# A two-layer attention and mixture-of-experts kernel: the second layer norm moved into the expert rounds, and the next stage's preparation into the last of them

## The chip, the cores and the metric

The kernel runs on one core of one Trainium2 chip. The metric is the device time of one execution in microseconds (us); lower is better. The engines are named as the profile names them: PE is TensorE's matmul, PEld its weight load, DVE is VectorE, ACT is ScalarE, POOL is GpSimd, SP is SyncE, which here only starts transfers.

## What is computed

The input X is 16 sequences of 256 rows of 128 numbers. Two layers are applied, each of the same form (cut from the reference):

```python
x = L0_attn_x
xn = _layernorm(x, axis=-1)
s = _L0_attn_ref(xn, L0_attn_w_in, L0_attn_w_out)
g = _silu(_L0_ffn_ref(xn, ...))          # 8 experts, 2 chosen per row, and a shared one
x = x + s * g
xn = _layernorm(x, axis=-1)              # the second layer norm
s = _L1_attn_ref(xn, Wq, bq, Wk, bk, Wv, bv, Wo, bo, rel_bias)
g = _silu(_L1_ffn_ref(xn, ...))          # two layers of window attention and a gated MLP
x = x + s * g
```

`_layernorm` is `(x - mean) / sqrt(var + 1e-5)` over the 128 numbers of a row. `_L1_attn_ref` has 16 heads of 8 numbers; it adds to the scores a bias that depends on the distance of query and key, clipped at 128, so the bias of all heads is a table of 256 x 256 per head.

## The kernel before

X and Y (the normalised rows) stay in SBUF as 32 tiles of 128 rows. Five stages follow one another, each a block in which every engine has a program of its own, written out by hand with semaphores; a block ends when all engines are done: `front` (first layer norm and router), `window_attention` (up to 262 us in the profile), `experts` (to 524 us), `normalise` (the second layer norm, to 533.5 us), `bias_attention` (to 909 us) and `inner_layers` (to the end).

**experts** works through 8 rounds of 512 rows (4 tiles). A round has 14 steps, one for each slice of 128 of the 1,760 hidden features (the last has 96). In a step, PE makes the gate product and the up product (three matmuls each, since every operand is split in a high and a low part) and, for the slice three steps back, the down product; ACT takes Silu of the gate (`e_sg`, L1202) and rounds the previous slice's product to its high part (`e_hh`, L1210); DVE multiplies `e_sg` by the router's share (L1243, steps 0 to 10 only; both inputs in SBUF) and with the up product in PSUM (L1247, which makes `e_h`); POOL makes the low part of `e_hh` (L1223; both inputs in SBUF). PE's up product of step s waits for `e_h` of step s-2, since they share a bank. At step 5 of a round DVE also updates the rows of the round before (L1250, L1253) and takes their statistics (L1257); at step 8 it splits the next round's input (L1231), which SP has fetched from Y. Rounds 1 to 6 stand in a hardware loop; round 0, round 7 and the rest after it (part 8, which updates the last 4 tiles) are written out.

**normalise** turns all 32 tiles' statistics into means and inverse deviations (L200 to L226) and then scales the 32 tiles, 16 on DVE (L454) and 16 on ACT (L445). Meanwhile SP loads the weights of the next stage and the bias table (4 MB in two transfers, L125).

**bias_attention** first transposes its weights and prepares constants (PE L839 to L844, ACT L929 and L931, DVE L984 to L996), then the first sequence's queries and keys (PE L852, L856; ACT L939 to L945; POOL L810, `a_kM`, the keys masked per head). Then it runs over 128 units of 4 heads x 128 queries x 256 keys: PE scores of two units (L884, into the four banks 0 to 3, so it waits until DVE has read them), DVE adds the table (L1004) and takes row maxima (L1008), POOL subtracts them (L816), ACT exponentiates, PE transposes and sums. A step of the written-out program is a unit; DVE and the scores work on even steps, two units at a time, four units ahead. Aux products run between: `x`, `qk`, `v` per sequence, `d` and `y` per tile (DVE L1015 and L1017 take the results).

Of the kernel before, what the change touches and what calls it, by code (L numbers as in the profile page):

```python
# [13 lines left out]
P = 128  # L14
# [63 lines left out]
def build_kernel(nc, t, out):  # L78
    ctx = ExitStack()
    with ctx:  # L80
# [6 lines left out]
        stats = ctx.enter_context(nc.sbuf_tensor("ln1_stats", [P, NT, 6], F32))  # L87
        with ExitStack() as early:
            S = early.enter_context(nc.sbuf_tensor("S0", [P, NT, P], F32))
            chosen = early.enter_context(nc.sbuf_tensor("chosen", [P, NT // 4, NE, 4], F32))  # L90
            wgu = early.enter_context(nc.sbuf_tensor("wgu", [P, 2, FEAT], F32))
            wd = early.enter_context(nc.sbuf_tensor("wd", [P, len(chunks(FEAT)), P], F32))
            experts_loaded = early.enter_context(nc.semaphore("experts_loaded"))

            with ExitStack() as first:
                sb = lambda n, s: first.enter_context(nc.sbuf_tensor("a0_" + n, s, F32))
                attn = {"wT": sb("wT", [P, 4, P]), "own": sb("own", [P, 4]), "table": sb("table", [P, TPB, H, 2 * WIN]),
                        "loaded": first.enter_context(nc.semaphore("a0_loaded"))}
                route = router_buffers(nc, first)
                front(nc, t, ps, X, Y, ident, wgu, wd, experts_loaded, skew, attn, route)  # L100
                window_attention(nc, "a0", t, ps, ident, Y, S, attn, lambda dve, part: choose_experts(nc, dve, part, route, chosen))
            experts(nc, t, ps, ident, X, Y, S, chosen, (wgu, wd, experts_loaded), stats)
        weights = inner_weights(nc, ctx)
        with ExitStack() as late:
            S = late.enter_context(nc.sbuf_tensor("S1", [P, NT, P], F32))
            table = late.enter_context(nc.sbuf_tensor("a1_table", [P, TPB, H, SEQ], F32))
            table_loaded = late.enter_context(nc.semaphore("a1_table_loaded"))
            attn = bias_weights(nc, late)
# [12 lines left out]
def load_bias_table(sp, skew, table, loaded):  # L121

    for tile in range(TPB):
        src = bass.AP(tensor=skew.tensor, offset=skew.offset + P * tile, ap=[[1, P], [512, H], [1, SEQ]])
        sp.dma_start(table[:, tile], src).then_inc(loaded, 16)  # L125
# [2031 lines left out]
```

## Time and profile before

| | |
|---|---|
| median of 3 runs | 1678.47 us (1676.99 to 1678.49) |
| the profiled execution | 1676.0 us, of which the profile's span is 1674.2 us |
| busy share of the span | PE 89%, DVE 79%, ACT 72%, POOL 66%, weight loads 69% |
| TensorE's granted clock, mean | 0.958 of 2.4 GHz |
| experts, 250 to 480 us | PE 213.8 of 230 us busy, DVE 149.1, POOL 123.6 |
| bias attention, 560 to 920 us | PE 332.3 of 360 us busy, DVE 321.1, POOL 288.8 |

A busy share is a mean over stages; what a change in one stage costs has to be read from the rows of that stage. Times in rows are in us from the start of the span unless marked ns. "Idle before" names how long the engine had waited and what ended the wait.

### The profile page before, as it was taken

Reading aid. Unit: us, or ns where it says so; the run is one execution under the profiler, and the core shown is the slowest. Engines: PE = TensorE matmul, PEld = TensorE weight load, DVE = VectorE, ACT = ScalarE, POOL = GpSimd, SP = SyncE. Lnnn points to the kernel's source line nnn. Section 1 sums busy time; section 2 is a strip of 40 time slices with the busy share of each in tenths; the row PEclk is TensorE's granted clock in tenths of the full one; section 3 lists DMA queues with packets and bytes.
Section 4 is the critical chain, followed back from the end, with each engine's and each line's share of the span. In section 5 each row is a group of like instructions: output and inputs, shape, how many; then the busy total and the mean of one; then the engine's idle time right before and its main releaser. Section 6 shows DMA issues by size and latency. Waiting matters only on the chain. (4 is left out here: it accounts for less than half of the span.)

```text
span 1674.2 us, 43938 instructions
## 1 busy us (share of the span) xinstructions
PE 1482.3 (89%) x16870; PEld 1161.5 (69%) x16870; DVE 1321.7 (79%) x2179; ACT 1212.5 (72%) x2057; POOL 1100.9 (66%) x659
## 2 busy tenths in 40 slices
PE   6899996999995899999997588999999999989885
PEld 5577774888883566666665377777777777777774
DVE  4898884667665999999996888888888888888753
ACT  2677774555554688888886488888888888888863
POOL 2677761666663788888886576776677766766615
PEclk7899997999997899999998799999999999999997
DMA  5000004333323200000000001011111111111113
GB/s 175 2 4 3 3 3 124 113 97 106 99 69 113 78 2 14 2 14 2 14 2 23 10 21 34 22 26 28 27 27 27 27 27 24 27 27 27 24 24 107
DMA packets 66432, 66.79 MB, mean 40 GB/s; under 512 B 26252, under 2 KB 46256, under 8 KB 65984
## 3 DMA queue, kind: packets, MB, share of 16 engines
q1 hardware_dynamic: 66240, 64.13, 13.7%
q8 instruction: 132, 2.16, 0.5%
q14 instruction: 60, 0.49, 0.1%
HBM read 40.69 MB, written 4.36 MB: 27 GB/s over the span
## 5 line engine op out<-in xcount | busy, mean ns | idle before, releaser
L816 POOL TENSOR_TENSOR a_prob<-a_prob,a_top 128x1024 f32<-128x1024 f32 x128 | 239.7, 1894 | 48.3 <-DVE a_top L1008 48.3
L1223 POOL TENSOR_TENSOR e_hh<-e_h,e_hh 128x512 fp32r<-128x512 f32 x112 | 148.8, 1329 | 121.4 <-ACT e_hh L1210 121.2
L1491 POOL TENSOR_TENSOR i_qk<-i_qk,i_rt 128x1024 f32<-128x1024 f32 x64 | 152.0, 2374 | 39.4 <-DVE i_rt L1940 35.0
L1501 POOL TENSOR_TENSOR i_qk<-i_qk,i_rn 128x1024 f32<-128x1024 f32 x64 | 122.5, 1915 | 79.9 <-DVE i_rn L1919 79.9
L1796 ACT ACTIVATE i_prob<-i_prob,i_top 128x128 f32<-128x128 f32 x512 | 156.4, 392 | 17.2 <-DVE i_top L1928 15.3
L1004 DVE TENSOR_TENSOR a_prob<-ps,a_table 128x1024 f32<-128x1024 f32 x128 | 149.7, 1211 | 23.0 <-PE ps L884 21.0
L962 ACT ACTIVATE a_probT<-ps 128x1024 f32<-128x1024 f32 x128 | 131.1, 1025 | 44.5 <-PE ps L892 44.5
L892 PEld LDWEIGHTS ps<-ident,a_prob 128*128 128x128 f32 x1024 | 112.8, 141 | 64.2 <-ACT a_probT L962 50.7
L1488 POOL TENSOR_TENSOR i_qk<-i_raw,i_rot 128x1024 f32<-128x1024 f32 x59 | 140.2, 2376 | 23.8 <-issue 23.8
L1008 DVE TENSOR_REDUCE a_top<-a_prob 128x4 f32<-128x1024 f32 x128 | 149.4, 1208 | 0.0
L892 PE MATMUL ps<-ident,a_prob 128*128 128x128 f32 x1024 | 138.3, 278 | 6.0 <-ACT a_probT L962 1.6
L537 POOL TENSOR_TENSOR a_prob<-a_prob,a_top 128x1024 f32<-128x1024 f32 x64 | 120.2, 1897 | 26.2 <-DVE a_top L690 26.2
L1202 ACT ACTIVATE e_sg<-ps 128x512 f32<-128x512 f32 x112 | 66.8, 597 | 96.0 <-PE ps L1129 95.2
L957 ACT ACTIVATE a_prob<-a_prob 128x1024 f32<-128x1024 f32 x128 | 135.5, 1058 | 0.6 <-POOL a_prob L816 0.6
L1761 ACT ACTIVATE i_raw<-ps 128x1024 f32<-128x1024 f32 x64 | 65.6, 1025 | 76.1 <-PE ps L1558 75.9
L1247 DVE TENSOR_TENSOR e_h<-ps,e_sg 128x512 f32<-128x512 f32 x112 | 77.5, 692 | 41.6 <-PE ps L1129 27.0
L1127 PE MATMUL ps<-e_xT,e_wgu_hi 128*128 128x512 f32 x224 | 90.1, 402 | 10.7 <-DVE e_wd_lo L1269 10.7
L1243 DVE TENSOR_TENSOR e_sg<-e_sg,e_share 128x512 f32<-128x512 f32 x88 | 68.1, 773 | 33.5 <-ACT e_sg L1202 32.8
L1129 PE MATMUL ps<-e_xT,e_wgu_lo 128*128 128x512 f32 x224 | 89.1, 398 | 0.0
L1128 PE MATMUL ps<-e_xT,e_wgu_hi 128*128 128x512 f32 x224 | 88.5, 395 | 0.0
L1637 PE MATMUL ps<-i_wo,i_oT 128*128 128x128 f32 x512 | 71.0, 283 | 19.6 <-ACT i_oT L1807 19.6
L1940 DVE TENSOR_TENSOR i_rt<-ps,i_rot 128x512 f32<-128x512 f32 x128 | 81.9, 682 | 6.4 <-ACT i_raw L1761 6.4
(297 smaller groups left out, 4296.7 us busy)
## 6 DMA issues: line engine op xcount, KB each, us to landing
i_V<-i_V SPq DMA_DIRECT2D x96, 130.0 KB, 2.3
e_share<-chosen_scratch SPq DMA_DIRECT2D x32, 256.0 KB, 3.2
a_table<-skew_scratch SPq DMA_DIRECT2D x2, 2048.0 KB, 12.4
e_share<-chosen_scratch SPq DMA_DIRECT2D x16, 224.0 KB, 2.9
e_share<-chosen_scratch SPq DMA_DIRECT2D x16, 192.0 KB, 2.7
e_share<-chosen_scratch SPq DMA_DIRECT2D x16, 160.0 KB, 2.5
X<-in_L_attn_x SPq DMA_DIRECT2D x4, 512.0 KB, 5.9
a_table<-in_c_l_table SPq DMA_DIRECT2D x1, 2048.0 KB, 7.9
```

The source lines that it names most:

```text
L537: nc.gpsimd.tensor_tensor(s, s, top[:, slot].unsqueeze(2).broadcast_to([P, HG, KW]), ALU.subtract).then_inc(shifted, 1)
L816: nc.gpsimd.tensor_tensor(s, s, top[:, slot].unsqueeze(2).broadcast_to([P, HG, KW]), ALU.subtract).then_inc(shifted, 1)
L892: last = nc.tensor.transpose(ps[:, 4 + b // 4, b % 4 * P:(b % 4 + 1) * P], flat[:, b * P:(b + 1) * P], ident[:, :])
L957: nc.scalar.activation(s, s, ACT.Exp).then_inc(exped, 1)
L962: nc.scalar.activation(probT[:, n % 4].rearrange('p (b n) -> p b n', b=2), ps[:, 4:6, :], ACT.Copy).then_inc(pT_sb, 1)
L1004: nc.vector.tensor_tensor(prob[:, slot].rearrange('p (b x) k -> p b x k', b=2), ps[:, 2 * (n % 2):2 * (n % 2) + 2, :].rearrange('p b (x k) ...
L1008: nc.vector.tensor_reduce(top[:, slot], prob[:, slot], AX.X, ALU.max).then_inc(max_done, 1)
L1223: nc.gpsimd.tensor_tensor(low, h[0:n, slot(b, parity, HBUF), :], high.bitcast(F32), ALU.subtract).then_inc(h_lo, 1)
L1488: nc.gpsimd.tensor_tensor(s, raw[:, T % 2], cosines, ALU.mult).then_inc(cos_done, 1)
L1491: nc.gpsimd.tensor_tensor(s, s, rt[:], ALU.add).then_inc(rotated, 1)
L1501: nc.gpsimd.tensor_tensor(flat, flat, rn[:, T // TPB % 2, T % TPB].unsqueeze(2).broadcast_to([P, 2 * FH, FD]), ALU.mult).then_inc(qk_done, 1)
L1796: last = nc.scalar.activation(s, s, ACT.Exp, bias=top[:, T % 2, h:h + 1])
```

## The change

1. `normalise` is gone. In `experts`, DVE keeps statistics of the 4 tiles of one round only; it takes them at step 6, turns them into variances and a first guess of the inverse deviation at step 7, refines the guess three times (twice at step 11, once at step 12: nine operations on 4 numbers a partition) and scales the four tiles at steps 12 and 13, all for the round before, in rounds 1 to 7. The first guess is now an integer trick on DVE, no longer Ln and Exp on ACT.
2. The last 4 tiles are normalised inside `bias_attention`, on DVE, at its steps 21, 23 and 25.
3. The weights and half the bias table are loaded in round 0 of the experts, over the room of the experts' raw weights, which are no longer needed there. In round 7 PE, ACT, DVE and POOL prepare the constants, the first sequence's queries and keys and `a_kM`.
4. `bias_attention` begins with the first scores (its step -4); the table's other half is loaded at its start.

The core of the diff (loads in `bias_weights`, names, and the parts removed from `bias_attention`, which the list above names, are cut):

```diff
+def small_variances(nc, dve, stats, mv, var, rstd):
+
+    for k in range(4):
+        nc.vector.bn_aggr(mv[:, k, :], stats[:, k, :])
+    dve.drain()
+    nc.vector.tensor_scalar(var[:], mv[:, :, 1], 1e-5, None, ALU.add)
+    dve.drain()
+    nc.vector.tensor_scalar(rstd[:].bitcast(I32), var[:].bitcast(I32), -0.5, RSQRT_MAGIC, ALU.mult, ALU.add)
+    dve.drain()
+
+
+def small_refinement(nc, dve, var, rstd, tmp):
+
+    nc.vector.scalar_tensor_tensor(tmp[:], var[:], -0.5, rstd[:], ALU.mult, ALU.mult)
+    dve.drain()
+    nc.vector.tensor_tensor(tmp[:], tmp[:], rstd[:], ALU.mult)
+    dve.drain()
+    nc.vector.scalar_tensor_tensor(rstd[:], tmp[:], 1.5, rstd[:], ALU.add, ALU.mult)
+    dve.drain()
...
@@ bias_attention @@
+        LAST_ROWS = 21
+        JOBS = sorted([(i * U + AT[kind], 0, kind, i, 0) for i in range(NBATCH) for kind in AT if i or kind == 'v'] + ...
...
         def _(sp):
-            sp.wait_ge(w_loaded, NWL)
-            sp.wait_ge(b_loaded, NBL)
+            load_bias_tile(sp, skew, 1, tile1[:], table_loaded)
             loads(sp)
...
+                if step == LAST_ROWS:
+                    small_variances(nc, dve, stats, mv, var, rstd)
+                    small_refinement(nc, dve, var, rstd, tmp)
+                if step == LAST_ROWS + 2:
+                    small_refinement(nc, dve, var, rstd, tmp)
+                    small_refinement(nc, dve, var, rstd, tmp)
+                if step == LAST_ROWS + 4:
+                    for k in range(4):
+                        r = NT - 4 + k
+                        last = nc.vector.tensor_scalar(Y[:, r, :], X[:, r, :], mv[:, k, 0:1], rstd[:, k:k + 1], ALU.subtract, ALU.mult)
+                    last.then_inc(last_rows, 1)
...
@@ experts, SP, after the shares of round 0 @@
+            sp.wait_ge(w_hi, 2)
+            sp.wait_ge(w_lo, 3)
+            load_bias_weights(sp, t, attn)
+            load_bias_tile(sp, skew, 0, attn["tile0"], attn["table_loaded"])
             with sp.Fori(1, ROUNDS) as i:
...
@@ experts, PE, in round 7 @@
+                if s == 1:
+                    pe.wait_ge(attn["w_loaded"], BIAS_LOADS)
+                    for j in range(4):
+                        last = nc.tensor.transpose(ps[:, TURNED, j * P:(j + 1) * P], wnat[:, j, :], ident[:, :])
...
+                elif s == OUT:
+                    pe.wait_ge(prep_sb, 2)
+                    nc.tensor.matmul(ps[:, TURNED, P:2 * P], bvT, wT[:, 3, :], start=True, stop=True).then_inc(prep_ps, 1)
+                    for k in range(TPB):
+                        last = nc.tensor.transpose(ps[:, 7, k * P:(k + 1) * P], Y[:, k, :], ident[:, :])
...
+                elif s == FETCH:
+                    pe.wait_ge(prep_sb, 3)
+                    for j, turned in enumerate((xT1, xR1)):
+                        last = nc.tensor.matmul(ps[:, 7, j * SEQ:(j + 1) * SEQ], wT[:, j, :], turned[:, 0, :], start=True, stop=True)
...
@@ experts, POOL, in round 7 @@
+                        if ending(i) and b == FETCH + 1:
+                            pool.wait_ge(prep_sb, 4)
+                            nc.gpsimd.tensor_tensor(kM1[:, 0], kT1[:, :].unsqueeze(1).broadcast_to([P, 4, SEQ]),
+                                                    own.unsqueeze(2).broadcast_to([P, 4, SEQ]), ALU.mult)
...
@@ experts, DVE @@
+                    if s == OUT + (exists(i) and 1) and exists(i - 1):
                         for k in range(4):
-                            nc.vector.bn_stats(stats[:, bass.ds(i * 4 - 4 + k, 1), :], X[:, bass.ds(i * 4 - 4 + k, 1), :])
+                            nc.vector.bn_stats(stats[:, k, :], X[:, bass.ds(i * 4 - 4 + k, 1), :].rearrange("p k e -> p (k e)"))
+                    if exists(i) and exists(i - 1):
+                        if s == OUT + 2:
+                            dve.drain()
+                            small_variances(nc, dve, stats, mv, var, rstd)
+                        elif s in (NR, NR + 1):
+                            small_refinement(nc, dve, var, rstd, tmp)
+                            if s == NR:
+                                small_refinement(nc, dve, var, rstd, tmp)
+                        if s in (NR + 1, NR + 2):
+                            for k in range(2):
+                                q = 2 * (s - NR - 1) + k
...
+                                nc.vector.tensor_scalar(to, own_rows, mv[:, q, 0:1], rstd[:, q:q + 1], ALU.subtract, ALU.mult)
```

In this code OUT is 5, FETCH is 8 and NR is 11.

The order of instructions shows where these land. On DVE in round 7, around the update of the previous round's rows (steps 5 to 8), the kernel before has:

```order
L1250 TENSOR_TENSOR e_upd<-ps,S 128x512 [waits e_out_T]
L1253 TENSOR_TENSOR X<-X,e_upd 128x512
L1257 BN_STATS ln_stats<-X 128x6 x4
L1243 TENSOR_TENSOR e_sg<-e_sg,e_share 128x512 [waits e_share_in1,e_gate_sb]
L1247 TENSOR_TENSOR e_h<-ps,e_sg 128x512 [waits e_h_lo,e_up_ps]
L1243 TENSOR_TENSOR e_sg<-e_sg,e_share 128x512 [waits e_gate_sb]
L1247 TENSOR_TENSOR e_h<-ps,e_sg 128x512 [waits e_h_lo,e_up_ps]
```

and the changed kernel:

```order
L1281 TENSOR_TENSOR e_upd<-ps,S 128x512 [waits e_out_T]
L1284 TENSOR_TENSOR X<-X,e_upd 128x512
L1274 TENSOR_TENSOR e_sg<-e_sg,e_share 128x512 [waits e_share_in1,e_gate_sb]
L1278 TENSOR_TENSOR e_h<-ps,e_sg 128x512 [waits e_h_lo,e_up_ps]
L1289 BN_STATS ln_stats<-X 128x6 x4
L1274 TENSOR_TENSOR e_sg<-e_sg,e_share 128x512 [waits e_gate_sb]
L1278 TENSOR_TENSOR e_h<-ps,e_sg 128x512 [waits e_h_lo,e_up_ps]
L436 BN_AGGR e_mv<-ln_stats 128x2 x4
L438 TENSOR_SCALAR e_var<-e_mv 128x4
L440 TENSOR_SCALAR e_rstd<-e_var 128x4
L1274 TENSOR_TENSOR e_sg<-e_sg,e_share 128x512 [waits e_gate_sb]
L1278 TENSOR_TENSOR e_h<-ps,e_sg 128x512 [waits e_h_lo,e_up_ps]
```

The statistics moved behind the share multiply and `e_h` of step 6, and the variances stand behind `e_h` of step 7.

On DVE at the end of the same round (steps 11 to 13), where the kernel before had three `e_h` operations and nothing between them, the changed kernel has:

```order
L1278 TENSOR_TENSOR e_h<-ps,e_sg 128x512 [waits e_h_lo,e_up_ps,e_gate_sb]
L446 SCALAR_TENSOR_TENSOR e_tmp<-e_var,e_rstd 128x4
L448 TENSOR_TENSOR e_tmp<-e_tmp,e_rstd 128x4
L450 SCALAR_TENSOR_TENSOR e_rstd<-e_tmp,e_rstd 128x4
L446 SCALAR_TENSOR_TENSOR e_tmp<-e_var,e_rstd 128x4
L448 TENSOR_TENSOR e_tmp<-e_tmp,e_rstd 128x4
L450 SCALAR_TENSOR_TENSOR e_rstd<-e_tmp,e_rstd 128x4
L1278 TENSOR_TENSOR e_h<-ps,e_sg 128x512 [waits e_h_lo,e_up_ps,e_gate_sb]
```

After these come three more small operations and two scalings, the `e_h` of step 13 and two more scalings, in each of the seven rounds.

On PE at the start of `bias_attention`, the kernel before has:

```order
L835 UNCONDITIONAL_BRANCH [waits barrier_Pool_Activation_PE_DVE_SP_release]
L839 MATMUL ps<-ident,a_wnat 128x128 [waits a1_w_loaded]
L839 MATMUL ps<-ident,a_wnat 128x128 x3
L842 MATMUL ps<-ident,a_bvo 128x128 [waits a1_b_loaded]
L844 MATMUL ps<-a_wT,a_bvT 128x128 [waits a1_wT_sb]
L852 MATMUL ps<-ident,Y 128x128 [waits a1_wO_sb]
L852 MATMUL ps<-ident,Y 128x128
L856 MATMUL ps<-a_xT,a_wT 128x256 [waits a1_aux_free]
L856 MATMUL ps<-a_xR,a_wT 128x256
L884 MATMUL ps<-a_kM,a_qT 128x512 [waits a1_aux_free,a1_masked]
```

and the changed kernel:

```order
L818 UNCONDITIONAL_BRANCH [waits barrier_Pool_Activation_PE_DVE_SP_release]
L860 MATMUL ps<-a_kM,a_qT 128x512 x4
L837 MATMUL ps<-a_wT,a_xR 128x128 x2
L860 MATMUL ps<-a_kM,a_qT 128x512 [waits a1_biased]
L860 MATMUL ps<-a_kM,a_qT 128x512 x3
L827 MATMUL ps<-ident,Y 128x128 [waits a1_aux_free]
```

The first scores stand right behind the release of the block and wait for nothing.

## Rows read from the trace of the kernel before

**Rows 1.** Timeline from the end of the experts to the first scores and their use: start us, us, engine, line.

```profile
524.42 0.21 DVE L200 TENSOR_TENSOR ln_mean<-ln_stats 128x32 f32<-128x32 f32 x1 [0.30 <-PEq L1051]
...
527.27 6.26 ACT L445 ACTIVATE Y<-X,ln_shift,ln_rstd 128x128 f32<-128x128 f32 x16 [1.06 <-DVE ln_shift L226]
...
543.58 2.09 PE L884 MATMUL ps<-a_kM,a_qT 32*128 32x512 f32 x8 [2.63 <-POOL a_kM L810]
...
545.81 2.36 DVE L1004 TENSOR_TENSOR a_prob<-ps,a_table 128x1024 f32<-128x1024 f32 x2 [8.46 <-PE ps L884]
```

**Rows 2.** Window of PE's last work in the experts: length, busy us (count) of PE, PEld, DVE, ACT, POOL, granted clock, DMA share, GB/s.

```profile
520.00:524.00 4.00, 0.98 (x6) 0.42 (x4) 2.14 (x6) 0.60 (x1) 0.00 (x0) 0.94 0.00 0
```

**Rows 3.** Timeline of POOL, DVE and PE in steps 5 to 12 of one expert round.

```profile
381.70 1.30 POOL L1223 TENSOR_TENSOR e_hh<-e_h,e_hh 128x512 fp32r<-128x512 f32 x1 [1.22 <-ACT e_hh L1210]
381.78 0.98 DVE L1257 BATCH_NORM_STATS2 ln_stats<-X  x4 [0.19 <-issue]
382.69 0.86 DVE L1243 TENSOR_TENSOR e_sg<-e_sg,e_share 128x512 f32<-128x512 f32 x1
...
384.45 0.50 PE L1127 MATMUL ps<-e_xT,e_wgu_hi 128*128 128x512 f32 x1
...
387.14 0.69 DVE L1247 TENSOR_TENSOR e_h<-ps,e_sg 128x512 f32<-128x512 f32 x1 [0.16 <-issue]
...
389.12 0.40 PE L1127 MATMUL ps<-e_xT,e_wgu_hi 128*128 128x512 f32 x1
...
394.25 0.69 DVE L1247 TENSOR_TENSOR e_h<-ps,e_sg 128x512 f32<-128x512 f32 x1 [1.40 <-PE ps L1129]
```

**Rows 4.** Timeline of DVE and POOL in the inner layers, where small DVE operations meet POOL.

```profile
933.80 2.34 POOL L1491 TENSOR_TENSOR i_qk<-i_qk,i_rt 128x1024 f32<-128x1024 f32 x1 [2.31 <-DVE i_rt L1940]
933.99 2.20 DVE L1917 TENSOR_TENSOR i_rtmp<-i_rtmp,i_rn 128x32 f32<-128x32 f32 x1
936.26 0.19 DVE L1919 SCALAR_TENSOR_TENSOR i_rn<-i_rtmp,i_rn 128x32 f32<-128x32 f32 x1
```

**Rows 5.** Two DVE lines over the whole run: duration ns least/median/most, first and last start.

```profile
L1998 DVE TENSOR_SCALAR i_var<-i_mv x16: 169/170/753, 1015.2 to 1644.5; 128x4 f32<-128x4 f32 x16
...
L2019 DVE TENSOR_SCALAR i_G<-i_ms,i_mv,i_rstd x60: 330/338/1176, 1024.2 to 1628.1; 128x128 f32<-128x128 f32 x60
```

**Rows 6.** Timeline of DVE near the end: the same small operations with POOL idle.

```profile
1644.09 0.38 DVE L1996 BATCH_NORM_AGGREGATE i_mv<-i_st 128x2 f32<-128x6 f32 x4
1644.55 0.17 DVE L1998 TENSOR_SCALAR i_var<-i_mv 128x4 f32<-128x4 f32 x1
...
1645.12 0.17 DVE L2012 SCALAR_TENSOR_TENSOR ps<-ps,i_rstd 128x4 f32<-128x4 f32 x1
1645.37 0.17 DVE L2014 TENSOR_TENSOR ps<-ps,i_rstd 128x4 f32<-128x4 f32 x1
...
1647.31 1.12 DVE L2019 TENSOR_SCALAR i_qk<-i_ms,i_mv,i_rstd 128x128 f32<-128x128 f32 x4
```

**Rows 7.** Timeline of POOL and DVE in the steady part of the bias attention.

```profile
603.24 3.74 POOL L816 TENSOR_TENSOR a_prob<-a_prob,a_top 128x1024 f32<-128x1024 f32 x2
...
605.85 2.33 DVE L1008 TENSOR_REDUCE a_top<-a_prob 128x4 f32<-128x1024 f32 x2
...
609.63 2.36 DVE L1004 TENSOR_TENSOR a_prob<-ps,a_table 128x1024 f32<-128x1024 f32 x2 [0.81 <-PE ps L884]
```

**Rows 8.** Timeline of PE: transposes in an expert round, and products of queries and keys.

```profile
378.49 0.60 PE L1153 MATMUL ps<-ident,e_gT 128*128 128x128 f32 x4
...
599.67 0.70 PE L856 MATMUL ps<-a_xT,a_wT 128*128 128x256 f32 x2
```

**Rows 9.** Timeline of DVE and ACT in round 0.

```profile
276.43 0.28 DVE L1269 TENSOR_TENSOR e_wd_lo<-wd,e_wd_hi 96x128 fp32r<-96x128 f32 x1
...
295.58 0.60 ACT L1190 ACTIVATE e_xT<-ps 128x512 fp32r<-128x512 f32 x1 [0.54 <-PE ps L1135]
```

**Rows 10.** The page's DMA issues: count, KB each, median us from issue to landing.

```profile
a_table<-skew_scratch SPq DMA_DIRECT2D x2, 2048.0 KB, 12.4
```

More of the change, by code:

```diff
@@ L86, in build_kernel @@
         skew = nc.dram_tensor("skew_scratch", (H, 512), F32, kind="Internal").ap()
[L87 to L108, printed above, removed]
-            normalise(nc, "ln1", X, Y, stats, lambda sp: (load_bias_weights(sp, t, attn), load_bias_table(sp, skew, table, table_loaded)))
-            bias_attention(nc, "a1", t, ps, ident, Y, S, attn, (table, table_loaded),
-                           lambda sp: load_inner_weights(sp, t, weights), kept)
+        stats = ctx.enter_context(nc.sbuf_tensor("ln1_stats", [P, 4, 6], F32))
@@ L717, in _, with bias_attention @@
                     between(dve, 1 + step // 8)
-def bias_attention(nc, name, t, ps, ident, Y, S, attn, bias=None, loads=None, kept=None):
+def bias_attention(nc, name, t, ps, ident, X, Y, S, stats, skew, attn, loads, kept):
     KW = SEQ
@@ L836, in _ @@
         def _(pe):
-            pe.wait_ge(w_loaded, NWL)
-            for j in range(4):
-                last = nc.tensor.transpose(ps[:, 0, j * P:(j + 1) * P], wnat[:, j, :], ident[:, :])
-            last.then_inc(wT_ps, 1)
-            pe.wait_ge(b_loaded, NBL)
-            nc.tensor.transpose(ps[:, 1, 0:P], bvo[:, 0, :], ident[:, :]).then_inc(wT_ps, 1)
-            pe.wait_ge(wT_sb, 2)
-            nc.tensor.matmul(ps[:, 2, 0:P], bvT[:, :], wT[:, 3, :], start=True, stop=True).then_inc(wT_ps, 1)
-            pe.wait_ge(wO_sb, 5)
             def job(n, kind, i, tile):
@@ L1064, in experts @@
         upd = sb("upd", [P, 4, P])
+        rows = gT[:, 0:2 * P].rearrange("p (v t) -> p v t", v=2)
+        mv, var, rstd, tmp = sb("mv", [P, 4, 2]), sb("var", [P, 4]), sb("rstd", [P, 4]), sb("tmp", [P, 4])
+        wnat, own, bqk, bvo, pick, bvT, parity_of, wT, wO, xT1, xR1, qT1, kT1, kM1 = (attn[n] for n in (
+            "wnat", "own", "bqk", "bvo", "pick", "bvT", "parity", "wT", "wO", "xT", "xR", "qT", "kT", "kM"))
         (rows_T, rows_sb, rows_out, w_hi, w_lo, staged, x_T, x_hi, x_lo, gate_ps, up_ps, gate_sb, shared_out, h1, h_hi,
```

209 lines of the change are left out of this document (120 added, 89 removed).

## The prediction

> **What bounds the kernel now.** I read four views, in this order. The timeline around the end of the experts shows the gap that the change wants to close: the next block's first instruction stands at 524.42, the scaling of the tiles fills ACT until 533.5, and the first scores start at 543.58, behind the preparation; DVE can add the bias at 545.81 [rows 1]. Between 524.4 and 543.6 nothing of the 128 units is done, so this stretch is on the path whole. The timeline of an expert round shows the price side. PE is never idle there: 14 steps of about 2.08 us and two sets of transposes make a round of 30.1. DVE has some 0.5 us to spare in a step with the share multiply and 1.40 in each of steps 11 to 13 [rows 3]. But in steps 6 to 10 it has nothing to spare: it is late by the update of step 5, and PE's up product of step 8 already comes 0.1 late (a first matmul of 0.50 where others take 0.40). `e_h` of step 8 ends at 387.83, and the up product that needs it starts at 389.12: 1.3 us of margin [rows 3]. In the bias attention DVE is the bound: two adds and two maxima take 4.6 us a pair of units, reciprocals and outputs 0.6 more, of a period of 5.5 (63 pairs between 545.8 and 891); it waits 0.81 us on one pair in two [rows 7].
>
> The third thing to see is how DVE and POOL meet. An operation on 32 numbers a partition, with both inputs in SBUF, took 2.20 us when POOL's multiply had started 0.19 before it, and ended 0.05 after POOL's did; its like took 0.19 with POOL idle [rows 4]. A sum on 4 numbers took 753 ns against 170, a scaling of 128x128 up to 1176 against 338 [rows 5]. The share multiply of step 6 took 0.86 instead of 0.69, because POOL had begun at 381.70 [rows 3]. So operations with two SBUF inputs, and scalings from SBUF to SBUF, stand still while POOL works. Operations that read PSUM, and the statistics, do not: 381.78 to 382.69 of statistics ran under POOL's 1.30 [rows 3].
>
> **What the change gives.** The first scores move from 543.58 to the start of the block, 524.45: **-19.1 us**. The adds follow at the same distance. PE's clock: its mean was 0.94 in 520 to 524, so it fell to 1.2 GHz just before 524 [rows 2], and the first scores run at 1.2 GHz before and after; no gain and no loss. POOL's clearing of V and ACT's table load move with the block and end before the first maxima exist. The table's first half is long there.
>
> **PE's preparation in round 7**: seven transposes at 0.10 to 0.15 us (four took 0.60 busy), one product like them, and two products of 256 columns (0.70 for the first) [rows 8], on an engine without idle time: **+2.0**.
>
> **The norm in rounds 1 to 7, on DVE.** Operations without POOL: aggregates 0.46, two sums 0.25 each, nine refinements at 0.25 apart, four scalings at 0.28 [rows 6], with drains 4.6 us a round. Two stretches:
> - Steps 6 to 10. The statistics, 0.9 us, stood in the shadow of POOL's operation; the share multiply of step 6 now meets POOL instead and ends when it did before, at 383.55, and the 0.9 comes on top. The variances add 1.05 at step 7, and one of their two sums meets POOL, about 1.1. Of 3.05, the margin of 1.3 takes part; PE loses 1.75.
> - Steps 11 to 13. Nine refinements and four scalings are 3.5 us. All wait for POOL, which has one operation of 1.3 per step; a wait of about 1.1 comes once for each of POOL's four operations from step 11 to the next round's step 0: 4.4. Free are 3 x 1.4 = 4.2 and a margin of some 2 us before PE's up products wait. 7.9 - 4.2 - 2.0 leaves 1.7.
>
> That is 3.5 a round, **+24.5** for seven. The bounds: nothing, if the waits fall between POOL's operations, and 5.0 a round, if more of the share multiplies, pushed out of their rhythm, meet POOL as well. I take 3.5, since the rows of steps 6 to 10 leave DVE no place to catch up.
>
> The Trainium skill, "VectorE: DVE Perf Modes", section "The TRN2 errata — SBUF-src ops pay a fixed extra latency per instruction", tabulates VectorE's SBUF operations at 58 cycles plus the elements, an estimate of 0.065 us for four numbers. By it eleven small operations a round would cost 2.0 us less than by their distance of 0.25 in rows 6, 14 us over seven rounds, and the whole sum would come out near +6. The trace decides here, with 0.17 us each and 0.25 apart [rows 6].
>
> **DVE's and POOL's preparation in round 7**: a fill, seven small copies, sums and scalings, 1.8 us in all, of which three meet POOL (3 x 1.1), and on POOL one more `a_kM` of the size of a subtraction, 1.9, in step 9. Of this 5 to 7 us the free 0.5 a step takes part: **+4** (0 to 7).
>
> **The last four tiles in the bias attention, on DVE.** 4.5 us of operations at the distances of rows 6. Each of the three places follows a pair of maxima, when POOL has just begun its two subtractions, 3.74 us in one piece [rows 7]. POOL starts them after the first maximum, DVE is done with the second 1.1 later, and then stands for the rest, less what fits between the two: about 2.1 a place, 6.3. DVE's own waits of 0.81 before the adds give back 2.4. **+8.4** (2 to 11).
>
> **Transfers.** SP's ten new transfers wait for DVE's splitting, which ends at 276.7; round 1's input is used at 295.6 [rows 9]. Nine small loads, the table of 2 MB and the input behind it fit into 19 us, since two such tables took 12.4 each to land when issued together [rows 10]. The second half starts at 524.4 and is needed at the fifth unit, 9 us after the first add, near 536. Both at nothing; late, they would cost up to 5.
>
> **The sum**: -19.1 + 2.0 + 24.5 + 4 + 8.4 = +19.8. On the profiled execution's 1676.0 that is 1695.8; the median of the runs shown is 2.5 above it. I predict **1697**, slower.
>
> **The rivals.**
> - **The small operations cost nothing** (faster). If they fall into POOL's pauses and DVE's spare time carries them, what remains is -19.1 + 2.0 and 2.1 for the last tiles: -15, 1662. For it: DVE is busy only 149 of 230 us in the experts. Against it: the busy share is not where the waits are, rows 3. It decides at the price of a round: with the other terms as above, below 0.7 us a round the change is faster; with those halved, below 1.5. Chance 0.15.
> - **Only the first stretch costs.** Steps 11 to 13 absorb theirs: 7 x 1.75 = 12, in place of 24.5, and 2 for the preparation: +5, 1681 to 1684. For it: 1.40 us free in each of the three steps. Chance 0.2, a quarter of it within 0.2% of no change.
> - **A transfer is late**: round 1's input or the second half of the table, up to 5 us over the forecast, 1702. Chance 0.05.
> - **The gap does not close**: the first adds wait for something else than the preparation, as the clearing of V or the landing of a table, and only some 10 us are won: 1706. For it: the rows show no execution in which the preparation is missing. Against: POOL waited for `a_kM`'s input, and PE for `a_kM` [rows 1]. Chance 0.05.
> - The forecast has the remaining 0.55.
>
> The Trainium skill, "SBUF — State Buffer", section "Who interferes with whom", says that VectorE and GpSimd share a pair of ports under an exclusive lock, that an instruction with two SBUF inputs or in a two-port mode takes it, and that the later one stands for the whole of the other's instruction. By that rule the sum is the +19.8; without it the price of a round falls to the 4.6 us of work, and the first rival comes near. The trace agrees with the rule: 2.20 against 0.19 us [rows 4].
>
> **The range.** Low, the second rival: 1680. High, 5.0 a round and the full 11 for the last tiles: 1696 + 10.5 + 2.6 with some of the late transfer, 1711. That leaves out the first rival and little else. 0.2% is 3.4 us, about what a measurement of this kernel can tell from no change. Faster by more 0.15, within it 0.05, slower by more 0.80.
>
> **What would show it.** In the changed profile: the first scores about 0.1 us after the last statistics of the experts (gain right); rounds 1 to 6 of 33 to 34 us where they were 30.1, with PE waiting for `e_h` at steps 9 to 10 and at the round's start; refinements of four numbers with a longest time over 1 us and a mean well above 0.17; the share multiply of step 6 near 1.7 us; the distance from the first add to the last one 6 to 11 us longer. Rounds of 30.5 or less would make the forecast wrong, and then most likely the sign. If the small operations show 0.17 us throughout, the waits for POOL were misjudged; if they wait but the rounds do not grow, it is the margins.

## The result, and the profile after

| | before | after |
|---|---|---|
| median of all runs shown | 1678.48 us (1676.99 to 1679.82) | 1692.22 us (1689.45 to 1693.08) |
| ratio, with its 95% interval | | 1.0079 [1.0062, 1.0097] |
| profiled execution, its span | 1676.0, 1674.2 | 1689.45, 1687.7 |
| DVE busy, POOL busy | 79%, 66% | 82%, 65% |

The changed kernel is slower by 0.8%, 13.7 us between the medians and 13.5 between the profiled executions. The forecast was 1697, with 1680 to 1711 as its range. The head of the changed kernel's page:

```profile
PE 1491.2 (88%) x16870; PEld 1164.3 (69%) x16870; DVE 1377.8 (82%) x2304; ACT 1205.8 (71%) x2039; POOL 1104.2 (65%) x659
```

**The gap closed.** The timeline of the changed kernel at the end of the experts, to be set against [rows 1] (start us, us, engine, line):

```profile
544.16 0.60 ACT L1204 ACTIVATE e_gT<-ps 128x512 f32<-128x512 f32 x1 [2.94 <-PE ps L1112]
544.81 1.11 PE L1136 MATMUL ps<-ident,e_gT 128*128 128x128 f32 x4 [0.69 <-ACT e_gT L1204]
...
548.79 2.09 PE L860 MATMUL ps<-a_kM,a_qT 32*128 32x512 f32 x8 [2.86 <-PEq L1019]
...
551.01 2.35 DVE L961 TENSOR_TENSOR a_prob<-ps,experts_then_bias 128x1024 f32<-128x1024 f32 x2 [2.53 <-PE ps L860]
```

The last Silu of the experts in the kernel before, where the same stretch began:

```profile
520.36 0.60 ACT L1197 ACTIVATE e_gT<-ps 128x512 f32<-128x512 f32 x1 [2.65 <-PE ps L1129]
```

From the experts' last Silu to the first scores it is now 4.63 us, and was 23.22 (520.36 to 543.58): 18.6 won. The first add follows the scores at 2.2 us, as before.

**The rounds grew.** The gate's Silu that opens rounds 2 and 3, in the kernel before and after:

```profile
337.54 0.60 ACT L1202 ACTIVATE e_sg<-ps 128x512 f32<-128x512 f32 x1 [1.04 <-PE ps L1129]
367.65 0.60 ACT L1202 ACTIVATE e_sg<-ps 128x512 f32<-128x512 f32 x1 [1.03 <-PE ps L1129]
```

```profile
341.68 0.58 ACT L1209 ACTIVATE e_sg<-ps 128x512 f32<-128x512 f32 x1
374.56 0.58 ACT L1209 ACTIVATE e_sg<-ps 128x512 f32<-128x512 f32 x1
```

Round 2, of 30.11 us, has become one of 32.88. Measured so for every round, and cut at the events that both kernels have, the 13.5 us come from these places:

| stretch | before | after | difference |
|---|---|---|---|
| to the first gate of round 0 (same code) | 278.62 | 280.82 | +2.2 |
| rounds 0 to 6 | 209.37 | 224.64 | +15.3 |
| round 7, to the last output's Silu | 32.37 | 38.70 | +6.3 |
| to the first scores | 23.22 | 4.63 | -18.6 |
| first add to last add of the bias attention | 345.32 | 355.62 | +10.3 |
| last add to the end (same code) | 783.1 | 781.0 | -2.1 |

The first and the last stretch are code that the change leaves alone. Over the profiles of all kernels of this document the first lies between 273.8 and 281.8 us and the last between 780.9 and 785.5, so nothing shows that the +2.2 and the -2.1 come from the change.

**Where a round loses.** Two places. Steps 6 to 10 of round 3 in the changed kernel, to be set against [rows 3]:

```profile
389.38 1.29 POOL L1250 TENSOR_TENSOR e_hh<-e_h,e_hh 128x512 fp32r<-128x512 f32 x1 [1.23 <-ACT e_hh L1217]
389.52 1.69 DVE L1274 TENSOR_TENSOR e_sg<-e_sg,e_share 128x512 f32<-128x512 f32 x1 [0.26 <-issue]
...
391.98 0.86 DVE L1289 BATCH_NORM_STATS2 ln_stats<-X 128x6 f32 x4
...
395.03 1.29 POOL L1250 TENSOR_TENSOR e_hh<-e_h,e_hh 128x512 fp32r<-128x512 f32 x1 [0.44 <-ACT e_hh L1217]
395.08 1.27 DVE L440 TENSOR_SCALAR e_rstd<-e_var 128x4 int32<-128x4 int32 x1
...
397.35 0.69 DVE L1278 TENSOR_TENSOR e_h<-ps,e_sg 128x512 f32<-128x512 f32 x1 [0.16 <-issue]
...
398.10 0.50 PE L1110 MATMUL ps<-e_xT,e_wgu_hi 128*128 128x512 f32 x1 [1.13 <-DVE e_h L1278]
```

The share multiply of step 6 takes 1.69 where it took 0.86, because it now meets POOL's operation, which the statistics met before. The integer guess of step 7, four numbers, stands 1.27 for the whole of POOL's 1.29. PE, which never waited in the rounds before the change, waits 1.13: this is the up product of step 10, which needs the `e_h` of step 8. And the end of that round:

```profile
402.54 2.54 POOL L1250 TENSOR_TENSOR e_hh<-e_h,e_hh 128x512 fp32r<-128x512 f32 x2 [0.41 <-ACT e_hh L1217]
402.66 1.19 DVE L448 TENSOR_TENSOR e_tmp<-e_tmp,e_rstd 128x4 f32<-128x4 f32 x1 [0.20 <-issue]
403.93 1.18 DVE L450 SCALAR_TENSOR_TENSOR e_rstd<-e_tmp,e_rstd 128x4 f32<-128x4 f32 x1
...
407.44 1.68 DVE L1303 TENSOR_SCALAR Y<-X,e_mv,e_rstd  x2
407.49 1.29 POOL L1250 TENSOR_TENSOR e_hh<-e_h,e_hh 128x512 fp32r<-128x512 f32 x1 [2.41 <-ACT e_hh L1217]
409.04 0.68 DVE L1278 TENSOR_TENSOR e_h<-ps,e_sg 96x512 f32<-96x512 f32 x1
...
409.77 0.50 PE L1110 MATMUL ps<-e_xT,e_wgu_hi 128*128 128x512 f32 x1 [0.62 <-DVE e_h L1278]
```

Two of the nine refinement operations and one of the scalings stand for POOL; the `e_h` of step 13 is late and PE's up product waits 0.62 for it in the next round's step 1. Over all rounds the small operations took 21.4 us more than they would at their shortest durations, the scalings 7.6, the share multiplies 16.1 (8.1 before the change).

### The profile page after: what moved, and what is told of

It is laid out like the page before. It is cut to its first block and busy times, and to the rows that moved or that the text cites. A ratio compares the mean times of both kernels' runs of the same rounds, so it can differ in the third digit from the quotient of the medians.

```text
span 1687.7 us, 44126 instructions
## 1 busy us (share of the span) xinstructions
PE 1491.2 (88%) x16870; PEld 1164.3 (69%) x16870; DVE 1377.8 (82%) x2304; ACT 1205.8 (71%) x2039; POOL 1104.2 (65%) x659
## 5 line engine op out<-in xcount | busy, mean ns | idle before, releaser
L1217 ACT ACTIVATE e_hh<-e_h 128x512 fp32r<-128x512 f32 x112 | 70.5, 630 | 68.8 <-DVE e_h L1278 66.4
L1274 DVE TENSOR_TENSOR e_sg<-e_sg,e_share 128x512 f32<-128x512 f32 x88 | 75.4, 856 | 14.8 <-ACT e_sg L1209 12.0
```

## The experiments

In all of them the theory is that DVE's waits for POOL make the price of the moved norm; the rivals say what else could. Times are medians, each ratio with its 95% interval is against the kernel before on the same chip, and a "round" is the distance between first gates, taken from the run's profile.

### Small operations over PSUM; no norm in the rounds

`e1_psum_rounds`, in `experts`:

```diff
-        mv, var, rstd, tmp = sb("mv", [P, 4, 2]), sb("var", [P, 4]), sb("rstd", [P, 4]), sb("tmp", [P, 4])
+        mv, rstd = sb("mv", [P, 4, 2]), sb("rstd", [P, 4])
+        var, tmp = ps[:, GATED, 0:4], ps[:, GATED, 4:8]
```

> The changed kernel, but in the expert rounds the variance and the temporary of four numbers lie in PSUM (bank 4, after the update has read it), so that none of the eleven small operations has two SBUF operands; the scalings stay as they are. In the changed kernel the small operations of the rounds stood 21 us in all beyond their shortest durations, the scalings 7.6, the share multiplies 8. Theory (waits for POOL make the price of a round): no small operation of the rounds above 0.25 us, rounds 1 to 6 fall from 32.7 to between 30.8 and 31.8, the kernel is 7 to 13 us shorter, 1680 to 1685. Rival (the added work is the price, not the waits, or the waits fall where they cost nothing): rounds within 0.4 of 32.7, 1689 to 1692.

Measured: 1674.11 us, 0.9985 [0.9971, 0.9998], rounds 2 to 6 of 31.15 (32.75 in the changed kernel), round 7 of 34.15 (38.70). The same lines of the two kernels over the whole run (duration ns least/median/most), first the changed kernel, then this one:

```profile
L440 DVE TENSOR_SCALAR e_rstd<-e_var x7: 170/1273/1274, 329.4 to 525.4; 128x4 int32<-128x4 int32 x7
L448 DVE TENSOR_TENSOR e_tmp<-e_tmp,e_rstd x21: 161/164/1190, 337.3 to 537.9; 128x4 f32<-128x4 f32 x21
```

```profile
L440 DVE TENSOR_SCALAR e_rstd<-ps x7: 161/163/164, 324.5 to 510.9; 128x4 int32<-128x4 int32 x7
L448 DVE TENSOR_TENSOR ps<-ps,e_rstd x21: 170/171/171, 332.0 to 520.6; 128x4 f32<-128x4 f32 x21
L450 DVE SCALAR_TENSOR_TENSOR e_rstd<-ps,e_rstd x21: 161/163/165, 332.3 to 520.9; 128x4 f32<-128x4 f32 x21
```

The same operations, in the same number and place, with one operand in another memory: none waits any more (the share multiplies and the scalings still do), and the rounds fall as the theory said. Most of the price was not their work but their waits. The kernel's gain is larger than expected: round 7 gives back 4.5 us and not 1.6, of which below, and of the 15.2 us between the two profiled executions 4.9 stand ahead of the first gate, where the code is the same.

`e2_no_norm_rounds` leaves out the small operations and the scalings in the rounds, so its result is not normalised:

```diff
-                    if exists(i) and exists(i - 1):
+                    if False:
                         if s == OUT + 2:
```

> The changed kernel without the small operations and the scalings of the second norm in the expert rounds (the first 28 tiles are not normalised); the statistics stay at step 6, the preparation in round 7 and the last four tiles stay. Theory: rounds 1 to 6 are back near 30.1 (30.1 to 30.6), round 7 is near 35, the kernel 18 to 20 us shorter, 1671 to 1675. Rival (the move of the statistics from step 5 to step 6, out of the shadow of POOL's operation, costs by itself the 0.9 us a round of the prediction): rounds near 31.0, 1678 to 1680.

Measured: 1668.55 us, 0.9953 [0.9936, 0.9969]; rounds 1 to 5 of 30.11 or 30.12 and round 7 of 34.16. The time lies below the expected 1671 to 1675, the rounds are as the theory had them. The whole growth of the rounds is that of the small operations and scalings, and the moved statistics alone cost nothing: a share multiply still takes up to 1.70 us there, but within the margin. The run also gives the preparation's own price: 34.16 - 32.37 = 1.8 us.

### Statistics back at step 5

`e6_stats_step5`:

```diff
-                    if s == OUT + (exists(i) and 1) and exists(i - 1):
+                    if s == OUT and exists(i - 1):
```

> The changed kernel with the statistics of a round back at step 5, where they stood before the change. The run without the norm had rounds of 30.12 with the statistics at step 6, so alone their move costs nothing. Theory A (it costs 0.9 us a round together with the variances, as the prediction had it: the share multiply of step 6 meets POOL's operation behind the update, and with statistics ahead of it that wait was hidden): rounds 1 to 6 fall by 0.7 to 1.0, to 31.7 to 32.0, the kernel 5 to 7 us shorter. Rival B (DVE recovers it before PE notices; the price comes from the waits of the small operations and scalings alone): rounds within 0.3 of 32.7.

Measured: 1682.47 us, 1.0027 [1.0013, 1.0041], rounds 2 to 6 of 31.00, a gain of 1.75 a round and more than either said. The integer guess at step 7 now meets POOL in one round of seven, not in six. All the small operations together still wait 17 us over the run, where it was 21: it is above all the place of a wait that has changed. What remains is the late end of the round alone: from the gate of step 0 to that of step 1 it is 3.05 us where it was 2.01, and from step 9 to step 10 it is 2.08 again (3.67 in the changed kernel). Round 7 gains nothing by it: it takes 39.88 us, and 38.70 in the changed kernel.

### The last four tiles

`e4_no_last_tiles`:

```diff
-                    if i >= NBATCH - 4 // TPB:
-                        pe.wait_ge(last_rows, 1)
...
-                if step == LAST_ROWS:
-                    small_variances(nc, dve, stats, mv, var, rstd)
-                    small_refinement(nc, dve, var, rstd, tmp)
...
```

> The changed kernel without the norm of the last four tiles (those are not normalised), and nothing else. Theory: from the first add to the last 345.3 us as before the change, the kernel 9 to 11 us shorter, 1681 to 1683. Rival (part of the 10.3 us comes from something else in the bias attention, as the halves of the table lying in two buffers or the later start of a transfer): the distance stays above 348 and the gain below 7.

Measured: 1679.16 us, 1.0012 [1.0000, 1.0023]; first to last add 345.33 us (345.32 before the change). The 10.3 us are these operations' whole; the kernel's time is 2 us below the expected 1681 to 1683. How they lose is in the changed kernel's timeline:

```profile
618.61 3.75 POOL L800 TENSOR_TENSOR a_prob<-a_prob,a_top 128x1024 f32<-128x1024 f32 x2 [1.83 <-DVE a_top L965]
...
620.02 0.51 DVE L438 TENSOR_SCALAR a_var<-a_mv 128x4 f32<-128x4 f32 x1
620.61 1.77 DVE L440 TENSOR_SCALAR a_rstd<-a_var 128x4 int32<-128x4 int32 x1
...
636.31 3.74 POOL L800 TENSOR_TENSOR a_prob<-a_prob,a_top 128x1024 f32<-128x1024 f32 x2
637.12 3.02 DVE L994 TENSOR_SCALAR Y<-X,a_mv,a_rstd 128x128 f32<-128x128 f32 x2
```

A blocked operation gets in when one of POOL's two subtractions ends, and the next one may be blocked by the second: the sum that makes the variance ends at 620.53, when the second subtraction has begun, and the guess behind it ends at 622.38, with that subtraction (618.61 + 3.75 = 622.36). Two scalings of 0.33 took 3.02.

`e5_last_tiles_before_maxima` puts the same three blocks (at steps 22, 24, 26) between the adds and the maxima:

```diff
                 if step % 2 == 0 and 0 <= n < UNITS:
                     add_bias(n, n % NBUF)
                     add_bias(n + 1, (n + 1) % NBUF)
+                if step == LAST_ROWS:
+                    small_variances(nc, dve, stats, mv, var, rstd)
+                    small_refinement(nc, dve, var, rstd, tmp)
...
                 if step % 2 == 0 and 0 <= n < UNITS:
                     row_max(n, n % NBUF)
```

> The changed kernel with the norm of the last four tiles in three places as before, but each between the second add of a pair and its first maximum, where POOL's two subtractions are nearly at their end, instead of behind the second maximum, where they have just begun. Same operations, same number in each place. Theory (the waits for POOL make over half of the 10.3 us of the bias attention): the waits fall from 6.8 us to under 1.5, the distance from the first to the last add is 348.5 to 350.5 (the work of 4.5 less some free time), the kernel 5 to 7 us shorter, 1685 to 1687. Rival (the work and its place in DVE's row is the price): the distance stays above 354.

Measured: 1684.66 us, 1.0044 [1.0026, 1.0061]; first to last add 350.51, within the expectation. The waits are 1.9 us, not under 1.5: POOL's `a_kM` was in the way once.

```profile
623.43 1.89 POOL L794 TENSOR_TENSOR a_kM<-a_kT,experts_then_bias 128x1024 f32<-128x1024 f32 x1
623.57 1.77 DVE L448 TENSOR_TENSOR a_tmp<-a_tmp,a_rstd 128x4 f32<-128x4 f32 x1
```

`e3_last_tiles_first` does all of it ahead of DVE's first add:

```diff
+            small_variances(nc, dve, stats, mv, var, rstd)
+            for _ in range(3):
+                small_refinement(nc, dve, var, rstd, tmp)
+            for k in range(4):
...
+            last.then_inc(last_rows, 1)
             dve.wait_ge(table_loaded, 16)
```

> The changed kernel with the norm of the last four tiles in one piece at the start of the bias attention, ahead of DVE's first add, where DVE is idle for 2.3 us and POOL only clears V. The same 4.5 us of DVE work. Theory (in the old place 6.8 us of waits for POOL's subtractions come on top of the 4.5 of work): the first add is 2 to 4 us later, the distance from the first to the last add falls from 355.6 to about 345.5, the kernel is 6 to 8 us shorter, 1684 to 1686. Rival (the work costs, not the waits; the clearing of V holds DVE just as the subtractions do): first add 5 us or more later, 1688 or more.

Measured: 1685.73 us, 1.0046 [1.0028, 1.0065]; first to last add 345.55, the first add 3.7 us later. The gain is 6.4 of the 10.3. POOL's clearing of V does hold DVE, as the rival had it, but only one operation of it: the variance, with one SBUF input.

```profile
549.83 2.23 POOL L786 MEMSET a_V<- 128x2560 f32 x1 [6.26 <-POOLq L1015]
549.88 0.38 DVE L436 BATCH_NORM_AGGREGATE a_mv<-ln_stats 128x2 f32<-128x6 f32 x4 [0.31 <-PEq L1015]
550.34 1.75 DVE L438 TENSOR_SCALAR a_var<-a_mv 128x4 f32<-128x4 f32 x1
```

### The remedies together

`e7_psum_spread` is `e1` with the last tiles' work in six pieces, one on every second pair of units, between adds and maxima:

```diff
+                if step == LAST_ROWS:
+                    small_variances(nc, dve, stats, mv, var, rstd)
+                if step in (LAST_ROWS + 4, LAST_ROWS + 8, LAST_ROWS + 12):
+                    small_refinement(nc, dve, var, rstd, tmp)
+                if step in (LAST_ROWS + 16, LAST_ROWS + 20):
...
```

> Small operations of the rounds over PSUM, and the norm of the last four tiles spread over six pairs of units in the bias attention, each piece between the adds and the maxima (variances, then three times one refinement, then twice two scalings, every second pair). Theory: rounds of 31.16 as in the run with PSUM, round 7 of 34.15, and the six pieces of 0.7 to 1.05 us go mostly into the 0.81 that DVE waits on one pair in two: distance from first to last add 345.5 to 348, and the kernel 7 to 10 us shorter than with PSUM alone, 1664 to 1668, faster than before the change by 10 or more. Rival (each place delays the next maximum and POOL after it, whatever its size): distance above 350, 1669 or more.

Measured: 1667.35 us, 0.9945 [0.9925, 0.9965]; rounds of 31.14, first to last add 347.0. The operations still wait 3.5 us for POOL there, but together with their work they cost 1.7 us; that DVE's free 0.81 us on one pair in two [rows 7] takes the rest is the reading, not tested by itself.

`e8_psum_spread_act` takes the scalings from DVE, which computes a shift instead, and adds on ACT:

```diff
+                    if s == NR + 2 and exists(i) and exists(i - 1):
+                        act.wait_ge(refined, i)
+                        for q in range(4):
...
+                            nc.scalar.activation(to, own_rows, ACT.Identity, bias=shift[:, q:q + 1], scale=rstd[:, q:q + 1])
```

> As the kernel with PSUM and spread pieces, and the four scalings of a round on ACT (Y = X * rstd + shift) at step 13 behind its copy, two small PSUM operations more on DVE. That takes 1.35 us of scalings and 0.83 of their waits from DVE in each round and puts four activations of some 0.3 us on ACT. Theory (what is left of the rounds' price, 1.04 us a round, is DVE being late through the scalings and the share multiplies that meet POOL behind them): rounds fall to between 30.1 and 30.6, the kernel 4 to 7 us shorter than without ACT's part, 1658 to 1663. Rival (ACT, with two activations of 1.2 us in a step of 2.08, becomes late by four more in one step and delays POOL's input and PE): rounds of 31.2 or more.

Measured: 1672.43 us, 0.9966 [0.9952, 0.9980]; rounds of 31.16. The theory fell: with the statistics at step 6, what is left of a round's price is not in the scalings. The median is 5 us above that of `e7`. From the first gate of the experts to their last Silu it is 250.6 us against 249.6, 1.0 longer; in the profiled executions most of the rest stands in the unchanged code at both ends. The rival's reason, that ACT delays PE, does not account for the rounds either, since with the statistics at step 5 (the next two runs) ACT's part leaves them at 30.1.

`e9_psum_stats5_spread` is `e7` with the edit of `e6`; `e10_psum_stats5_spread_act` is `e8` with it.

> As the kernel with PSUM and spread pieces, and the statistics of a round back at step 5. Measured so far, per round over the 30.11 of before: 2.65 with both as in the change, 0.9 with the statistics at step 5 alone, 1.05 with PSUM alone. Theory A (two lateness terms that add: the share multiply of step 6 meets POOL when the statistics don't stand between, and the small operations meet it later): both remedies together leave 0 to 0.3, rounds 30.1 to 30.4, the kernel 5 to 7 us shorter than with the statistics at step 6, 1659 to 1663. Rival B (both cure the same lateness, and what is left is the added work of DVE in steps 5 to 8): rounds stay at 30.8 to 31.2, 1665 to 1668.

Measured: 1664.59 us, 0.9919 [0.9896, 0.9941], rounds 1 to 5 of 30.11 to 30.15: the norm is in the rounds and costs nothing there. That is theory A for the rounds; the time lies 1.6 us above its range, and round 7, of 35.99 us, is 1.8 longer than in `e7` (34.19).

> As the run before it, and the four scalings on ACT at step 13. With the statistics at step 6 ACT's part changed the rounds by +0.05 us (31.19 against 31.14), so steps 11 to 13 hold no price once the small operations do not wait. Theory A: rounds within 0.15 of the run before it, time the same within 2 us. Rival B (the scalings, with 0.83 us of waits a round, are what is left of the price when steps 5 to 8 are cured): rounds 0.3 or more shorter, down to 30.1.

Measured: 1663.99 us, 0.9924 [0.9903, 0.9946], rounds 2 to 6 of 30.11 to 30.15. Theory A again: ACT's part does neither good nor harm in these rounds. At the end of round 7 it helps: from the last gate to the last Silu it is 5.57 us (6.51 in `e9`), and the experts from first gate to last Silu are 0.9 shorter, too little to see in the medians.

PE's first product of each gate and up set and its waits for `e_h`, from 280 to 480 us, in the changed kernel, in `e7` and in `e9`, one fence each (count; busy us, mean ns; idle us before and the releaser):

```profile
L1110 PE MATMUL ps<-e_xT,e_wgu_hi 128*128 128x512 f32 (+1 forms) x175 | 71.6, 409 | 9.5 <-DVE e_h L1278 9.3
```

```profile
L1111 PE MATMUL ps<-e_xT,e_wgu_hi 128*128 128x512 f32 (+1 forms) x183 | 73.3, 400 | 4.0 <-DVE e_h L1279 4.0
```

```profile
L1111 PE MATMUL ps<-e_xT,e_wgu_hi 128*128 128x512 f32 (+1 forms) x187 | 75.0, 401 | 0.0
```

The mean of rounds 2 to 6 in the four combinations (30.09 before the change):

| | small operations over SBUF | over PSUM |
|---|---|---|
| statistics at step 6 | 32.75 | 31.15 |
| statistics at step 5 | 31.00 | 30.10 |

So there are two latenesses, and PE's own waits for `e_h` show where each falls. In a round of the changed kernel PE waits 1.13 us at step 10, and 0.13 to 0.31 and 0.64 at steps 0 and 1 of the next round. In `e1` the second wait is gone and 0.8 of the first is left; in `e6` the first is gone and 0.5 to 0.64 of the second is left; in `e9` there is none. The late end of the round costs 0.9 by itself (31.00 - 30.10), the steps 6 to 10 cost 1.05 by themselves (31.15 - 30.10), with two share multiplies that meet POOL (1.69 and 1.49 us in a round of `e1`). Both together cost 2.65, and the 0.7 above the sum belongs to neither alone: with the statistics at step 6 the guess meets POOL as well, and PE waits longer at both places.

**Round 7.** In `e9` its end is late by itself: 6.51 us from the last gate to the last Silu (4.76 before the change, 8.66 in the changed kernel), with two scalings of 2.63 us ahead of the last `e_h`. `e11_early_in_round_7` moves that round's refinements and scalings one step forward:

```diff
-                        elif s in (NR, NR + 1):
+                        elif s in (NR - ending(i), NR + 1 - ending(i)):
...
-                        if s in (NR + 1, NR + 2):
+                        if s in (NR + 1 - ending(i), NR + 2 - ending(i)):
```

> As the kernel with PSUM, statistics at step 5 and spread pieces, and in round 7 alone the refinements and scalings one step earlier (steps 10 to 12 in place of 11 to 13). In that kernel's round 7 the time from the last gate on ACT to the last output's Silu was 6.51 us where it was 4.76 before the change, because two scalings, together 2.63 us in place of 0.6, stood ahead of the last product of step 13. Theory (what is late at the end of the experts goes onto the path whole): that time is 4.8 to 5.2 again, round 7 falls from 36.0 to 34.2 to 34.6, the kernel some 1.5 us shorter, 1661 to 1665. Rival (POOL's row is late by itself there, through the masking of the keys in step 9): the time stays at 6.0 or more.

Measured: 1663.15 us, 0.9918 [0.9896, 0.9940], but that time is 6.84: the theory fell. By the rows, the masking of the keys is in POOL's row there, POOL works nearly without a pause behind it, and the scalings meet it one step earlier instead, which is what the rival had:

```profile
514.82 1.90 POOL L1254 TENSOR_TENSOR a_kM<-a_kT,experts_then_bias 128x1024 f32<-128x1024 f32 x1
...
516.67 2.54 POOL L1251 TENSOR_TENSOR e_hh<-e_h,e_hh 128x512 fp32r<-128x512 f32 x2
...
517.33 1.97 DVE L1304 TENSOR_SCALAR Y<-X,e_mv,e_rstd 128x128 f32<-128x128 f32 x2
519.22 0.68 DVE L1279 TENSOR_TENSOR e_h<-ps,e_sg 128x512 f32<-128x512 f32 x1
```

What removes these last 2 us of round 7 was not found. Two runs point at ways that were not tried: in `e1` and `e7`, with the norm and the masking in round 7 but the statistics at step 6, this time is 4.76 and 4.80, so round 7 alone could keep its statistics there; and with the scalings on ACT (`e10`) it is 5.57. `e9`, `e10` and `e11` cannot be told apart by their times; each beats the kernel before by 0.8%. Of the 18.6 us that the closed gap gives, `e9` keeps 13: round 7 takes 3.6 and the last tiles 1.7.

## Why the prediction was right, term by term

| term | predicted | measured |
|---|---|---|
| first scores move | -19.1 | -18.6 |
| PE's preparation, and DVE's and POOL's | +2.0 and +4 | +1.8 for both |
| norm in seven rounds | +24.5 | +19.8 (15.3 in rounds 1 to 6 and, in round 7, 4.5) |
| last four tiles | +8.4 | +10.3 |
| transfers | 0 | 0 |
| unchanged code | 0 | +2.2 and -2.1 |
| sum | +19.8 | +13.5 |

- **The number.** The sum was 6.3 us too high: the preparation was put 4.2 too high, the norm 4.7, the last tiles 1.9 too low. The larger errors went the same way, towards too slow; the measured 1692 lies in the range, 5 us below the forecast. The 2.5 us between the profiled execution and the median was added only by half (1695.8 became 1697 and not 1698).
- **The sign** rested on one reading: that small SBUF operations stand for POOL, and that rows of steps 6 to 10 leave DVE no place to catch up. Both held. By PSUM against SBUF (`e1`) and by place against place (`e5`, `e6`, `e9`) it was the waits and not the work. The rival "small operations cost nothing" is what `e9` is, by another arrangement: 1664.6, where the rival was priced at 1662.
- **First stretch, 1.75 a round**: taking the statistics back to step 5 gives 1.75 (`e6`), but that the two numbers are equal is luck: with the small operations over PSUM the same move gives 1.05. The details came as told: the share multiply of step 6 at 1.69 (forecast "near 1.7"), the guess of step 7 waiting 1.1, PE waiting for `e_h` at step 10. The 0.9 of the statistics costs nothing alone (`e2`), as the prediction's own margin of 1.3 would have it. What it did not see is that the statistics' place also decides whether the guess, or the share multiply of step 8, meets POOL; so taking them back gave more than 0.9.
- **Second stretch, 1.7 a round**: 0.9 in rounds 1 to 6 if the first stretch is cured (31.00 against 30.10), 1.6 if it is not (32.75 against 31.15). Both stretches together were put at 3.5 and measured 2.65, and this is the mis-sized term. The step that was off was "a wait of about 1.1 comes once for each of POOL's four operations": in the rows of round 3 three operations waited (1.0, 1.0 and 1.1 beyond their own durations), 3.1 us in place of 4.4.
- **Round 7** went the other way: the norm cost 4.5 there where 3.5 was forecast. Of this 3.9 stand behind the last gate (4.76 us before, 8.66 after, from last gate to last Silu): behind the last `e_h` no margin follows, so all its lateness is on the path. And PE's clock fell: the last three products, before and after the change, begin with

```profile
519.36 0.50 PE L1127 MATMUL ps<-e_hh,e_wd_hi 96*128 96x512 f32 x1 [0.27 <-POOL e_hh L1223]
```

```profile
542.61 0.66 PE L1110 MATMUL ps<-e_hh,e_wd_hi 96*128 96x512 f32 x1 [1.71 <-POOL e_hh L1250]
```

  They take 0.96 us before, at a granted clock of 1.00, and 1.52 after, at a mean of 0.56: it had fallen to 0.50 (1.2 GHz) by 543.0, once PE had waited 2.40 and 1.71 us for POOL. That is 0.56 of the 3.9, and the prediction had no such term.
- **The preparation, PE's +2.0 and DVE's and POOL's +4**: 1.8 for all three together (`e2`). No run takes them apart; PE's products alone were put at 2.0, so little or nothing is left for DVE and POOL. That DVE's free 0.5 us a step took it all fits, but was not tested. POOL's masking of the keys did not show beside the norm in `e1` and `e7` (round 7 of 34.15 and 34.19, as without the norm), but with the statistics at step 5 round 7 was 1.8 longer (`e9`).
- **Last four tiles, +8.4**: 10.3. The waits were 6.8 us (6.3 forecast), the work 4.5; the 2.4 that DVE's own waits were to give back gave back only 1. Each place lies on one pair, and a pair has at most 0.81 free [rows 7], which may be the reason.
- **First scores, -19.1**: 18.6. PE's transposes behind the last Silu took 1.11 us against 0.66, because the granted clock was already 0.50 there and had been 1.00; the end of the experts lost 0.45 by it.
- **The transfers** were at nothing, and cost nothing: round 0 takes 28.86 us (28.83 before), and DVE's waits before its adds end with PE's scores, not with the table.

The Trainium skill, "SBUF — State Buffer", section "Who interferes with whom", has a VectorE instruction with at most one SBUF input, outside the two-port modes, not contend with GpSimd. By that rule `e1` had to work, and its trace agrees: an integer guess that read PSUM took 0.16 us with POOL's 1.30 begun 0.05 before it (386.87 in `e1`). In the changed kernel the same guess, also with a single SBUF input, did stand for POOL; the section counts `tensor_scalar` among the operations that can enter a two-port mode, and no run here shows which mode it was in.

## What to carry to other kernels

Before DVE work is put "into the free time" of a stage where POOL runs, count how many of its instructions have two SBUF inputs or scale from SBUF to SBUF: each can cost a whole POOL operation, whatever its own size. Put one operand into a corner of a free PSUM bank, and place what cannot be changed where POOL pauses; here these two, the first in the rounds and the second in the rounds and at the last four tiles, took a change from 0.8% slower to 0.8% faster with the same work. An operation that is free in a repeated round can be dear in the last one, where nothing follows that takes up the delay.

## What the runs showed that was not expected

- The place of an operation that never waits decides whether others do: four statistics (0.9 us, never blocked) in front of the share multiply or behind it change the round by 1.75 us, as they shift the share multiply of step 6 and the guess onto POOL's operations (in `e1`, by 1.05, that multiply and the one of step 8).
- A blocked operation of four numbers ends 0.02 to 0.05 us after POOL's, so that its own 0.16 us lie inside the wait; a blocked product of 128x512 ends some 0.5 us after POOL's (389.38 + 1.29 = 390.67 against 391.21).
- POOL's `MEMSET` held a DVE sum with one SBUF input and an SBUF output for 1.75 us (`e3`). The guess of `e1`, with a PSUM input and an SBUF output, never waited for POOL's subtractions; against `MEMSET` that form was not tried.
- The first gate of the experts, behind code that none of these kernels changes, stood anywhere between 273.8 and 281.8 us:

```profile
273.81 0.60 ACT L1209 ACTIVATE e_sg<-ps 128x512 f32<-128x512 f32 x1 [8.43 <-PE ps L1112]
```

```profile
281.84 0.60 ACT L1205 ACTIVATE e_sg<-ps 128x512 f32<-128x512 f32 x1 [8.44 <-PE ps L1108]
```

The first row is of `e5`, the second of `e3`. So single executions differ by up to 8 us before the changed part begins, while rounds 1 to 6 agree within 0.1 us between kernels of the same arrangement (`e3`, `e4`, `e5` and the changed kernel). Effects of 1 to 5 us were read from distances inside the trace for that reason; what makes the beginning vary was not looked into.
